# A two-layer block on one core: the down products of the shared gated block as fp32r parts with 512 tokens moving, placed three exponentials behind their rounding

## The chip, the core and the metric

The kernel runs on one core of one Trainium2 chip. The metric is the device time of one execution in microseconds (us), as the median of several runs. A core has five engines that run their own instruction streams in order and meet at semaphores: TensorE (PE, matrix products into PSUM), VectorE (DVE), ScalarE (ACT), GpSimd (POOL) and SyncE (SP, which issues most DMAs).

## What is computed

Two layers over 1024 tokens (batch 2, 512 tokens each) of width 256. The part that matters here is the first layer:

```
xn = layernorm(x)
s  = attention(xn)              # 16 heads of 16, 4 key-value heads, softmax over 512 keys
gate_up = xn @ w_gate_up.T      # 256 -> 2 x 1024
h  = silu(gate) * up            # 1024 wide
f  = h @ w_down.T               # 1024 -> 256, "down"
```

The result f is gated (its tanh is taken and the product scaled by it) and multiplied by the attention output; the sum with x goes to the second layer: a linear attention branch and a mixture of eight experts. All data are float32.

## The kernel before

The time is spent in three parts. A start (to about 45 us) loads, normalizes and projects. A long middle part (to about 221 us) does the attention of the first layer and, mixed into it, the shared gated block. The rest (112 us) is the second layer with the expert tiles.

**The middle part.** Attention runs over 8 units (2 batches x 4 key-value heads) of 4 steps with 4 products each, 128 in all. The plan calls each of these a `prob`: one PE product (L1749) whose 128x512 result ACT turns into exponentials (L1019). They are numbered 1 to 128 here, and "exponential 23" means the `prob` of that number and what stands behind it up to the next. Two PSUM banks serve them in turn, so the product of number q waits for the exponential of number q-2. The four products of a step with the values (`values`, L1759) stand behind the second exponential of the next step. Beside them run the `score` products (L1727) of the next unit, whose row maxima DVE takes (L1292), with two banks as well, and transposes of the second batch's query and key parts (`stack_T`, L1661, copied by ACT at L1027, in exponentials 20 to 42).

**The fill.** The shared block is cut into small items that stand between those of attention. For each batch and each of 8 slices of 128 hidden features: `gate` and `up`, two items each (L1816). An item is three products in fp32r, a rounded form of float32: the operands are split into a high part (rounded by ACT) and a low part (the difference, taken by POOL or DVE), and high x high, high x low and low x high are summed, each with 128 weights columns standing and 512 tokens moving. Then ACT takes the tanh (L1054), DVE makes `gated` (L1337) and `hidden` (L1348), which leaves hT, the hidden values with features in the partitions. After the 8 slices come the `down` items: 4 token tiles per batch x 8 slices, 64 in all, each one plain float32 product (L1829) with 128 tokens of hT standing and the 256 columns of the weight wdn moving. The trace shows such a float32 product as two matrix instructions. At the end of a token tile ACT takes tanh (L1063, 128x256) and DVE the product into gx (L1356, 128x256).

**What sets the order.** `attention_plan` writes one list that PE, ACT and DVE all walk. In it `put` places an item of attention and, ahead of it, items of the fill, as long as the fill is behind a pace (cost units spent, evenly over the 128 exponentials) or while a rough clock of the three engines says that the attention item would wait. POOL has its own code: it clears buffers, prepares the second batch's parts, takes the low parts of xnT (L803) and issues the scatter of rows (L836). SP walks loads and stores.

The lines around the change:

```
for j in range(TB):
    fill += [("down", b * TB + j, i) for i in range(NI)]
...
while fill and (spent < pace - SLACK or spent < pace + AHEAD and clock.start(item) > clock.now["pe"] + 0.1
...
if n >= 2 and hh == 0:
    act.wait_ge(s["values_done"], n - 1)
nc.scalar.activation(probs[:, n % 2, hh, :], ps[:, 2 + hh % 2, :], ACT.Exp,
```

## Time and profile before

| | us |
|---|---|
| median of 3 runs (336.23 to 338.54) | 336.7 |
| the profiled execution's own time | 335.74 |
| its span, first to last instruction | 333.5 |
| PE busy in the span | 317.5 (95%) |
| DVE busy | 223.9 (67%) |
| ACT busy | 161.4 (48%) |
| POOL busy | 66.9 (20%) |

Time outside the span is 2.2 us. In the views, an instruction's duration includes its way through the engine, so two that follow each other closely overlap; what a queue costs is read from the distance between starts, or from a row in which several are merged. The chain of waits gives PE's pieces by that distance. "x8" behind a group counts instructions.

### The profile page before, as it was taken

How to read it: one execution, taken by the hardware profiler on the slowest of the kernel's cores; microseconds unless marked ns; L12 is line 12 of the kernel's file. 1: busy time of each engine (PE TensorE's matmuls, PEld its weight loads, DVE VectorE, ACT ScalarE, POOL GpSimd, SP SyncE). 2: the span in 40 equal slices, each digit the busy share in tenths (PEclk: the TensorE clock that was granted, in tenths of full speed). 3: DMA queues.
4: the chain of work that ended last, by engine and by line, in shares of the span. 5: the costliest groups of instructions: out<-in, count | busy, mean ns of one | idle time of the engine just before them, and what ended most of it. 6: DMA issues, size and time to landing. Idle time of an engine off the chain costs nothing.

```text
span 333.5 us, 4912 instructions
## 1 busy us (share of the span) xinstructions
PE 317.5 (95%) x1646; PEld 189.5 (57%) x1646; DVE 223.9 (67%) x489; ACT 161.4 (48%) x299; POOL 66.9 (20%) x90
## 2 busy tenths in 40 slices
PE   8889999999999999999999999999999999999990
PEld 8655564455555545465455456546654677665650
DVE  3978968695566667868976772129899666454972
ACT  1794457566768455544384455532406622233230
POOL 5009633700030000000000002200321441116132
PEclk9999999999999999999999999999999999999997
DMA  7910073091280650400000005106944896034721
GB/s 221 422 41 0 0 151 108 4 221 37 65 192 3 130 129 9 118 2 2 0 3 1 0 2 206 48 2 249 375 166 115 317 428 264 16 129 145 249 92 36
DMA packets 19867, 39.19 MB, mean 118 GB/s; under 512 B 1698, under 2 KB 15235, under 8 KB 18688
## 3 DMA queue, kind: packets, MB, share of 16 engines
q1 hardware_dynamic: 18448, 35.69, 33.6%
q0 software_dynamic: 1392, 3.15, 2.7%
q8 instruction: 15, 0.25, 0.3%
q14 instruction: 12, 0.10, 0.1%
HBM read 34.02 MB, written 15.22 MB: 148 GB/s over the span
## 4 chain that ended last, share of the span: by engine, by line
PE 83%; DVE 11%; issue 2%; DMA 1%; ACT 1%; POOL 0%; SPq 0%; DVEq 0%; POOLq 0%
PE ps L1816 10%; PE ps L1759 9%; PE ps L1727 9%; PE ps L1829 8%; PE ps L1749 8%; PE ps L1871 6%; PE ps L1887 6%; PE ps L1899 6%; PE ps L1628 4%; PE ps L1564 3%; DVE nmax L1292 3%; PE ps L1661 3%; PE ps L1936 2%; PE ps L1607 2%; PE ps L1861 1%
## 5 line engine op out<-in xcount | busy, mean ns | idle before, releaser
L1292 DVE TENSOR_REDUCE nmax<-ps 128x1 f32<-128x512 f32 x128 | 85.2, 687 | 36.4 <-PE ps L1727 35.3
L1019 ACT ACTIVATE shared<-ps 128x512 f32<-128x512 f32 x128 | 73.8, 594 | 43.1 <-PE ps L1749 42.1
L1727 PE MATMUL ps<-experts 96*128 96x512 bf16 x128 | 47.8, 384 | 2.4 <-DVE experts L1299 1.1
L1749 PE MATMUL ps<-experts 99*128 99x512 bf16 x128 | 48.3, 383 | 0.0
L1829 PE MATMUL ps<-shared,experts 128*128 128x256 f32 x128 | 37.7, 386 | 0.2 <-DVE gated L1337 0.2
L1759 PE MATMUL ps<-shared,experts 128*32 128x512 f32 x256 | 34.1, 605 | 0.3 <-ACT shared L1019 0.3
L1727 PEld LDWEIGHTS ps<-experts 96*128 96x128 bf16 x128 | 12.4, 98 | 37.4 <-DVE nmax L1292 20.3
L1829 PEld LDWEIGHTS ps<-shared,experts 128*128 128x128 f32 x128 | 23.2, 191 | 8.7 <-issue 2.5
L1027 ACT ACTIVATE experts<-ps 96x1024 bf16<-96x1024 bf16 x18 | 18.3, 1021 | 9.8 <-PE ps L1661 9.6
L1628 PE MATMUL ps<-late_weights,xnT 128*128 128x512 f32 (+1 forms) x64 | 22.5, 492 | 0.4 <-DVE shared L1199 0.4
L1871 PE MATMUL ps<-experts,shared 128*128 x88 | 21.0, 382 | 0.8 <-ACT shared L1094 0.8
L1887 PE MATMUL ps<-experts,xsT 128*128 x44 | 20.9, 598 | 0.6 <-ACT xnT L1082 0.6
L836 POOL DMA_INDIRECT slot_rows<-xn,smi x8 | 9.2, 1151 | 57.9 <-DVE smi L1269 56.1
L1899 PE MATMUL ps<-experts,xsT 128*128 x44 | 20.8, 594 | 0.0
L1749 PEld LDWEIGHTS ps<-experts 99*128 99x128 bf16 x128 | 12.4, 98 | 11.5 <-issue 4.9
L1816 PE MATMUL ps<-xnT,late_weights 128*128 128x512 f32 x48 | 18.8, 392 | 0.0
L1871 PEld LDWEIGHTS ps<-experts,shared 128*128 128x128 f32 x88 | 15.9, 190 | 2.8 <-issue 1.0
L1054 ACT ACTIVATE tanh_g<-ps 128x512 f32<-128x512 f32 x16 | 9.5, 596 | 15.7 <-PE ps L1816 15.4
L1088 ACT ACTIVATE xsT<-ps 128x256 f32<-128x256 f32 x12 | 4.6, 384 | 24.1 <-PE ps L1853 24.1
L827 POOL TENSOR_TENSOR router_c<-router,small 128x16 f32<-128x16 f32 x1 | 0.2, 222 | 79.5 <-ACT small L1046 79.5
L1628 PEld LDWEIGHTS ps<-late_weights,xnT 128*128 128x128 f32 x64 | 11.5, 190 | 7.5 <-issue 6.1
L1100 ACT ACTIVATE late_weights<-late_weights 128x256 f32<-128x256 f32 x11 | 4.6, 415 | 21.1 <-DVE late_weights L1489 21.1
(236 smaller groups left out, 541.1 us busy)
## 6 DMA issues: line engine op xcount, KB each, us to landing
experts<-in_experts SPq DMA_DIRECT2D x8, 1536.0 KB, 12.0
slot_rows<-in_empty SPq DMA_DIRECT2D x4, 2080.0 KB, 11.5
shared<-in_wgu SPq DMA_DIRECT2D x2, 1024.0 KB, 9.1
shared<-in_wdn SPq DMA_DIRECT2D x1, 1024.0 KB, 11.4
expert_results<-in_empty SPq DMA_DIRECT2D x1, 1024.0 KB, 6.9
token_rows<-x SPq DMA_DIRECT2D x1, 1024.0 KB, 15.4
token_rows<-gx SPq DMA_DIRECT2D x1, 1024.0 KB, 4.5
shared<-expert_results SPq DMA_DIRECT2D x4, 256.0 KB, 5.6
```

Of the source, the lines that this page charges most:

```text
L1019: nc.scalar.activation(probs[:, n % 2, hh, :], ps[:, 2 + hh % 2, :], ACT.Exp, scale=float(HD) ** -0.5).then_inc(s["exp_done"], 1)
L1027: nc.scalar.activation(dst, src.rearrange("p (h s) -> p h s", h=2), ACT.Copy).then_inc(s["misc_free" if is_late(it) else "stack_copied"], 1)
L1292: nc.vector.tensor_reduce(nmax[:, 4 * t + hh:4 * t + hh + 1], ps[:, m % 2, :], AX, ALU.max, negate=True).then_inc(s["max_done"], 1)
L1628: last = nc.tensor.matmul(bank[:, a, 0:hi - lo], xnT[:, k, P * j:P * j + P], win[:, k, lo:hi], start=k == 0, stop=k == KD - 1)
L1727: nc.tensor.matmul(ps[:, m % 2, :], qs[0:KS, b, GR * g + hh, P * t:P * t + P], ks[0:KS, b, g, :], start=True, stop=True).then_inc(s["score ...
L1749: nc.tensor.matmul(ps[:, 2 + hh % 2, :], ks[0:KM, b, g, P * t:P * t + P], qs[0:KM, b, GR * g + hh, :], start=True, stop=True).then_inc(s[" ...
L1759: last = nc.tensor.matmul(ps[VW * hh:VW * hh + VW, 4, :], vaug[:, TB * b + t, g, :], probs[:, n % 2, hh, :], start=t == 0, stop=t == TB - 1)
L1816: ins = nc.tensor.matmul(ps[:, bk, :], w_parts[w_], x_parts[x_], start=k == 0 and n_ == 0, stop=k == KD - 1 and n_ == 2)
L1829: ins = nc.tensor.matmul(ps[:, bk, 0:D], hT[:, i, P * (j % TB):P * (j % TB) + P], wdn[:, i, :], start=i == 0, stop=i == NI - 1)
L1871: last = nc.tensor.matmul(ps[:, 6, 0:D], hmT[:, i % 2, P * k:P * k + P], Wm[:, bass.ds(base[i] + 2 * KD * EI + D * k, D)], start=k == 0, s ...
L1887: last = nc.tensor.matmul(ps[:, i % 2, :], xsT[:, i % 2, P * k:P * k + P], Wm[:, bass.ds(base[i] + EI * k, EI)], start=k == 0, stop=k == K ...
L1899: last = nc.tensor.matmul(ps[:, 2 + i % 2, :], xsT[:, i % 2, P * k:P * k + P], Wm[:, bass.ds(base[i] + EI * (KD + k), EI)], start=k == 0, ...
```

## The change

- Each `down` item becomes three fp32r products, with 128 columns of a weight part standing and the 512 tokens of a batch moving, as in `gate` and `up`. There are 2 column halves x 8 slices x 2 batches = 32 items. The result has features in the partitions.
- The weight wdn is split: ACT rounds it in two pieces (`round_down`, 128x1024 each), POOL takes the low parts. Each slice of hT is split (`h_parts`, 16 in all): ACT rounds 128x512, POOL takes the low part. Four high parts can be held at a time (PARTS), so from the fifth on the rounding waits for the items of four slices before.
- At a half's end ACT takes tanh of 128x512 and DVE the product, into `gated`. Then `back` items turn the result round: 4 transposes each, 16 in all, and ACT copies 128x512 into gx.
- In the plan, one `h_parts` is placed behind an exponential. A `down` item is let in only 3 exponentials behind the `h_parts` of its values (LAG), and `back` 3 behind the last `down`; while the first item of the fill isn't let in, none is. The pace is that of 120 exponentials instead of 128.
- POOL now walks the list too: its low parts of xnT, the router's centring and the first scatter stand at their places in it.
- Smaller edits: the 0.5 for PE's warm-up products is written by POOL instead of DVE; the bias addition at L1472 is followed by a wait for its own end instead of a wait at a later reader; two semaphores for stored tables are merged.

```diff
-        for j in range(TB):
-            fill += [("down", b * TB + j, i) for i in range(NI)]
-    cost = {"gate": 3, "up": 3, "down": 2}
+        fill += [("down", 2 * b + c, i) for i in range(NI) for c in range(2)]
+        fill += [("back", 2 * b + c, 0) for c in range(2)]
+    cost = {"gate": 3, "up": 3, "down": 3, "back": 3}
...
+    def ready(f):
+        if f[0] == "down":
+            return probs[0] - placed.get(NI * (f[1] // 2) + f[2], probs[0]) >= LAG
+        return f[0] != "back" or probs[0] - placed["down"] >= LAG
...
-        while fill and (spent < pace - SLACK or spent < pace + AHEAD and clock.start(item) > clock.now["pe"] + 0.1
+        while fill and ready(fill[0]) and (spent < pace - SLACK or spent < pace + AHEAD and clock.start(item) > clock.now["pe"] + 0.1
...
+        if coming and item[0] == "prob" and (item[1] % TB, item[2]) not in ((2, 1), (2, 2), (2, 3), (3, 0)):
+            part()
...
-            pace = start + (total - start) * (GR * n + hh + 1) / (GR * STEPS)
+            pace = start + (total - start) * (GR * n + hh + 1) / (GR * STEPS - 8)
...
+            def lower_h(c):
+                pool.wait_ge(s["h_high_ready"], c + 1)
+                b, i = divmod(c, NI)
+                nc.gpsimd.tensor_tensor(h_low(i), hT[:, i, :], h_high(b, i).bitcast(F32), ALU.subtract).then_inc(s["h_low_ready"], 1)
...
+                elif kind == "h_parts":
+                    b, i = divmod(it[1], NI)
+                    if i < PARTS:
+                        act.wait_ge(s["up_ready"], NI * (b + 1))
+                    else:
+                        act.wait_ge(s["down_ready"], 2 * (NI * b + i - PARTS + 1))
+                    bk, n = bank_use[("up", it[1])]
+                    act.wait_ge(free_sem[bk], n + 1)
+                    nc.scalar.activation(h_high(b, i), hT[:, i, :], ACT.Copy).then_inc(s["h_high_ready"], 1)
...
-                    nc.scalar.activation(gated[:, j % 2, 0:D], ps[:, 6 + j % 2, 0:D], ACT.Tanh, scale=0.25).then_inc(s["down_tanh"], 1)
+                    nc.scalar.activation(gated[:, c, :], ps[:, 6 + c, :], ACT.Tanh, scale=0.25).then_inc(s["down_tanh"], 1)
...
-                    ins = nc.tensor.matmul(ps[:, bk, 0:D], hT[:, i, P * (j % TB):P * (j % TB) + P], wdn[:, i, :],
-                                           start=i == 0, stop=i == NI - 1)
+                    if c == 0:
+                        pe.wait_ge(s["h_low_ready"], NI * b + i + 1)
+                    w_parts = [w[:, P * c:P * c + P] for w in (down_high(i), down_low(i))]
+                    h_parts = [h_high(b, i), h_low(i)]
+                    for n_, (w_, h_) in enumerate(((0, 0), (0, 1), (1, 0))):
+                        ins = nc.tensor.matmul(ps[:, bk, :], w_parts[w_], h_parts[h_], start=i == 0 and n_ == 0, stop=i == NI - 1 and n_ == 2)
...
+                    for a in range(2):
+                        for c in range(2):
+                            at_ = P * (2 * half + a)
+                            last = nc.tensor.transpose(ps[:, bk, P * (2 * a + c):P * (2 * a + c) + P], gated[:, c, at_:at_ + P], ident)
+                    last.then_inc(s["back_T"], 1)
...
-            nc.vector.tensor_tensor(qkv1[0][:, 1:TB, :], qkv1[0][:, 1:TB, :],
-                                    bin_b.rearrange("p (o n) -> p o n", o=1).to_broadcast([P, TB - 1, 3 * D]), ALU.add).then_inc(s["bias_added"], 1)
+            chain(nc.vector.tensor_tensor(qkv1[0][:, 1:TB, :], qkv1[0][:, 1:TB, :],
+                                          bin_b.rearrange("p (o n) -> p o n", o=1).to_broadcast([P, TB - 1, 3 * D]), ALU.add))
```

Three places show what moved. First PE around exponentials 23 to 27, before: L1749 is a `prob`, L1727 a `score`, L1661 a `stack_T`, L1829 a `down`, L1759 the `values`.

```order
L1749 MATMUL ps<-experts 128x512
L1727 MATMUL ps<-experts 128x512
L1749 MATMUL ps<-experts 128x512
L1727 MATMUL ps<-experts 128x512
L1829 MATMUL ps<-shared,experts 128x256
L1661 MATMUL ps<-identb,experts 96x128 x8
L1749 MATMUL ps<-experts 128x512
L1727 MATMUL ps<-experts 128x512
L1829 MATMUL ps<-shared,experts 128x256
L1749 MATMUL ps<-experts 128x512
L1759 MATMUL ps<-shared,experts 32x512 x4
```

The same place of the changed program, where L1846, L1824, L1758, L1929 and L1856 stand for these:

```order
L1846 MATMUL ps<-experts 128x512
L1824 MATMUL ps<-experts 128x512
L1846 MATMUL ps<-experts 128x512
L1824 MATMUL ps<-experts 128x512
L1758 MATMUL ps<-identb,experts 96x128 x8
L1846 MATMUL ps<-experts 128x512
L1824 MATMUL ps<-experts 128x512
L1846 MATMUL ps<-experts 128x512
L1929 MATMUL ps<-xn,gx 128x512
L1929 MATMUL ps<-experts,gx 128x512
L1929 MATMUL ps<-xn,shared 128x512
```

The first `down` moved from exponential 24 to 26, and exponentials 23 to 25 have no item of the fill.

Second, ACT at the same exponentials, before: L1019 is an exponential, L1027 the copy of a `stack_T`.

```order
L1027 ACTIVATE experts<-ps 96x1024
L1019 ACTIVATE shared<-ps 128x512 x2
L1027 ACTIVATE experts<-ps 96x1024
L1019 ACTIVATE shared<-ps 128x512 x2
L1027 ACTIVATE experts<-ps 96x1024
```

And changed, with L1123 the exponential, L1131 the copy, L1095 the rounding of a slice of hT:

```order
L1131 ACTIVATE experts<-ps 96x1024
L1123 ACTIVATE shared<-ps 128x512
L1095 ACTIVATE xn<-experts 128x512
L1123 ACTIVATE shared<-ps 128x512
L1095 ACTIVATE xn<-experts 128x512
L1131 ACTIVATE experts<-ps 96x1024
L1123 ACTIVATE shared<-ps 128x512
L1095 ACTIVATE xnT<-experts 128x512
L1123 ACTIVATE shared<-ps 128x512
L1131 ACTIVATE experts<-ps 96x1024
```

Three roundings now stand between the exponentials 23 to 26.

Third, PE at the end of the attention, exponentials 124 to 128, before (L1628 is the first product of the second layer):

```order
L1749 MATMUL ps<-experts 128x512
L1829 MATMUL ps<-shared,experts 128x256
L1749 MATMUL ps<-experts 128x512
L1829 MATMUL ps<-shared,experts 128x256
L1749 MATMUL ps<-experts 128x512
L1759 MATMUL ps<-shared,experts 32x512 x4
L1829 MATMUL ps<-shared,experts 128x256
L1749 MATMUL ps<-experts 128x512
L1829 MATMUL ps<-shared,experts 128x256
L1749 MATMUL ps<-experts 128x512
L1829 MATMUL ps<-shared,experts 128x256
L1759 MATMUL ps<-shared,experts 32x512 x4
```

And changed (L1704 is half of the attention's output product, L1725 stands for L1628):

```order
L1704 MATMUL ps<-wl,experts 128x256 x4
L1846 MATMUL ps<-experts 128x512 x2
L1856 MATMUL ps<-shared,experts 32x512 x4
L1846 MATMUL ps<-experts 128x512 x4
L1856 MATMUL ps<-shared,experts 32x512 x4
L1846 MATMUL ps<-experts 128x512 x2
L1856 MATMUL ps<-shared,experts 32x512 x4
L1725 MATMUL ps<-late_weights,xnT 128x512
```

Exponentials 121 to 128 had one `down` each and now have none.

## Rows read from the trace of the kernel before

**Rows 1.** The page: busy time of the engines, share of the span, instructions
```profile
PE 317.5 (95%) x1646; PEld 189.5 (57%) x1646; DVE 223.9 (67%) x489; ACT 161.4 (48%) x299; POOL 66.9 (20%) x90
```
**Rows 2.** The page: the chain that ended last, by engine
```profile
PE 83%; DVE 11%; issue 2%; DMA 1%; ACT 1%; POOL 0%; SPq 0%; DVEq 0%; POOLq 0%
```
**Rows 3.** Windows: stretch, its length, busy PE PEld DVE ACT POOL, PEclk, DMA
```profile
72.70:79.00 6.30, 6.25 (x48) 3.66 (x45) 5.04 (x10) 3.81 (x7) 0.00 (x0) 1.00 0.55 156
79.00:84.40 5.40, 5.40 (x44) 3.19 (x42) 2.90 (x8) 4.58 (x8) 0.00 (x0) 1.00 0.01 3
84.40:90.30 5.90, 5.90 (x39) 3.38 (x38) 2.45 (x5) 4.47 (x8) 0.00 (x0) 1.00 0.08 24
...
176.90:183.10 6.20, 6.04 (x32) 2.96 (x31) 3.82 (x6) 3.77 (x9) 0.22 (x1) 1.00 0.01 2
183.10:186.90 3.80, 3.67 (x20) 1.25 (x19) 2.83 (x6) 2.28 (x4) 0.00 (x0) 1.00 0.00 0
212.13:221.14 9.01, 8.76 (x49) 4.03 (x48) 0.84 (x2) 5.33 (x10) 0.00 (x0) 1.00 0.01 2
...
10.00:20.00 10.00, 8.15 (x35) 5.25 (x36) 8.09 (x28) 8.31 (x15) 0.00 (x0) 1.00 0.77 315
320.00:333.50 13.50, 5.00 (x24) 3.63 (x22) 5.19 (x11) 2.08 (x5) 5.08 (x5) 0.82 0.12 44
```
**Rows 4.** The chain of waits in order of time: start, us, what
```profile
88.24 0.45 PE ps L1661 x8
...
131.17 0.22 PE ps L1727
...
131.82 2.07 PE ps L1816 x9
...
200.66 2.16 PE ps L1829 x10
...
213.17 0.99 PE ps L1759 x8
...
214.79 0.22 PE ps L1749
...
220.10 0.04 issue
...
235.99 0.87 PE ps L1669 x8
...
241.16 2.46 DVE experts L1472
```
**Rows 5.** Groups of instructions by line and form
```profile
L1063 ACT ACTIVATE gated<-ps 128x256 f32<-128x256 f32 x8 | 3.0, 380 | 3.3 <-PE ps L1829 3.2
L954 ACT ACTIVATE late_weights<-shared 128x1024 fp32r<-128x1024 f32 x3 | 3.1, 1058 | 0.0
L958 ACT ACTIVATE experts<-xnT 128x512 fp32r<-128x512 f32 x2 | 1.2, 621 | 0.0
L803 POOL TENSOR_TENSOR xnT<-xnT,experts 128x512 fp32r<-128x512 f32 x2 | 2.5, 1275 | 28.7 <-ACT experts L958 28.7
L796 POOL TENSOR_TENSOR shared<-shared,xn 128x1024 fp32r<-128x1024 f32 x1 | 2.3, 2342 | 0.0
```
**Rows 6.** The timeline: start, us, what, number merged
```profile
87.65 0.38 PE L1749 MATMUL ps<-experts 99*128 99x512 bf16 x1
88.06 0.60 ACT L1019 ACTIVATE shared<-ps 128x512 f32<-128x512 f32 x1 [1.23 <-PE ps L1749]
205.07 1.08 ACT L1019 ACTIVATE shared<-ps 128x512 f32<-128x512 f32 x2 [0.91 <-PE ps L1749]
84.14 1.01 ACT L1027 ACTIVATE experts<-ps 96x1024 bf16<-96x1024 bf16 x1
85.05 0.59 ACT L1019 ACTIVATE shared<-ps 128x512 f32<-128x512 f32 x1
```
**Rows 7.** One tile's instructions, nres: duration ns min/median/max
```profile
L1327 DVE TENSOR_TENSOR nres<-nmax,mparts x8: 174/175/178, 39.1 to 196.8; 128x16 f32<-128x16 f32 x8
```

170 lines of the change are left out of this document (118 added, 52 removed).

## The prediction

> **What bounds the kernel now.** I read the page first. PE is busy for 317.5 of 333.5 us, DVE for 223.9, ACT for 161.4, POOL for 66.9 [rows 1]. The chain that ended last is PE for 83% and DVE for 11% [rows 2]. So PE's own work is nearly the time, and the question for every edit is how much PE work it takes away and how much new waiting it gives PE.
>
> Busy time alone doesn't tell waiting, since PE's instructions overlap. I therefore priced each item of the list by the chain's distances: a `prob` 0.22, a `score` 0.22, a `stack_T` 0.45, a step's `values` 0.99 [rows 4]. With ten matrix instructions of L1829 in 2.16 us, a `down` (two of them) is 0.43. With nine of L1816 in 2.07, a fp32r item of three is 0.69. Summed over the items that the plan puts there, exponentials 25 to 28 hold 5.2 us of PE work and took 5.40, 29 to 32 hold 5.7 and took 5.90, 21 to 24 hold 5.9 and took 6.30 [rows 3]. PE is full there; 0.2 us in four exponentials is lost, whatever stands in them. Only where the fill is thin is it more: 93 to 100 hold 9.0 and took 6.20 + 3.80 = 10.0 [rows 3].
>
> ACT is the engine to watch. In the same stretches it is busy 3.81 of 6.30, 4.58 of 5.40 and 4.47 of 5.90 us [rows 3], and the change gives it work exactly there.
>
> **The change, part by part.**
>
> *PE work.* Removed: 64 x 0.432 = 27.6 us. Added: 32 items x 0.69 = 22.1, and 16 float32 transposes at 0.109 (eight of L1669 in 0.87 [rows 4]) = 1.7. Sum: **-3.8 us**. The form of the new products (128 columns standing, 512 moving, fp32r) is that of L1816, so this price has its row; I give it 0.5 either way.
>
> *ACT.* A full queue costs less than durations: two exponentials together take 1.08 [rows 6], so 0.49 each and 0.10 once; a `stack_T` copy 0.91 (84.14 to 85.05 [rows 6]). The roundings are 0.62 each [rows 5], 0.52 in a queue. Added: 16 x 0.52 = 8.3, two of 1.06 for the weights [rows 5], about 1.9, four `back` copies 2.0. The tanhs stay even: 8 of 0.38 before [rows 5], 4 of 0.60 now. Together +12 us, which costs nothing by itself and everything where PE waits for the exponential behind it.
>
> *Where ACT is late: exponentials 23 to 26.* Before, a `down` stood in 24 and 25; now nothing does, and three roundings and two copies stand between the exponentials. ACT needs 4 x 0.49 + 3 x 0.52 + 2 x 0.91 = 5.3 us from the copy behind 22 to the rounding in 25; PE's items from 22 to 25 hold 4.4. I walked it, with an exponential starting 0.41 behind its product (87.65 to 88.06) and taking 0.60 [rows 6], and 0.04 for a signal [rows 4]. Zero is the product of 23. The copy of the last `stack_T` holds ACT to 1.1, exponential 23 ends at 1.6, the first rounding at 2.1, 24 at 2.6. PE, free at 1.3, waits for 23 until 1.65, and with product 26 for 24 from 2.1 to 2.65. POOL's part takes 1.28 [rows 5], so the first low part is there at 3.5, and the first `down`, due at 2.9, waits 0.6. That is 1.5 us. Further on, `max_rows` in 29 waits some 0.2 for a copy that the exponentials have pushed back; from 30 to 33 ACT's 5.4 and PE's 5.5 are level and the walk shows no more waits. Sum 1.7. A part of it replaces the 0.2 to 0.4 that four exponentials lose already, so I take **+1.4**. Bounds: 0, if every rounding fell into a gap of ACT, and 16 x 0.52 = 8.3, if PE waited for each (rival A).
>
> *The second half, 93 to 100.* Again there is no fill from 95 to 97. The walk gives waits of 0.2, 0.25 and 0.4 for exponentials and for DVE's maxima and 0.2 for the first low part, 1.05 in all, plus the usual 0.4: 1.45 against 1.0 lost before. **+0.4**.
>
> *Between last `down` and `back`, 46 to 49.* The fill is shut for three exponentials, `back` waits for tanh and DVE's product, and its two copies on ACT stand before exponential 50, for which product 52 waits. **+0.3**, between 0 and 1.
>
> *The tail, 121 to 128.* Eight `down`s left, 3.46 us of work. Before, this stretch to the last `values` took 9.01 [rows 3]. Without a fill it is bound by two banks and ACT: product, 0.41, 0.60 and 0.04 to the next product in that bank make 1.05. From the third product of a step at t: the fourth at t+0.22, the next step's first at 1.05, its second at 1.55 (ACT's queue), `values` 1.77 to 2.76, so 2.76 per step where PE's items are 1.88. From product 121: third at 1.43, 127 at 4.2, 128 at 4.4, its exponential ends at 5.7, `values` at 6.7. 9.0 - 6.7 = 2.3 gained of 3.46 removed here, so **+1.2** is given back. Bounds 0.8 and 1.7.
>
> *113 to 120.* Two `back` stand where PE waited before; +0.1.
>
> *Small edits.* The wait behind L1472 gives up its overlap with the next instruction of DVE, which is on the chain [rows 4]: +0.1. The 0.5 written by POOL and the merged signals stand before and behind longer waits: 0. POOL gets 16 x 1.28 + 2 x 2.34 = 25 us [rows 5] in a part of the program in which it is nearly idle (0.00 us busy in five of the six stretches from 72.7 to 221.1 [rows 3]); what waits for it is PE's `down`, counted above.
>
> Sum: -3.8 + 1.4 + 0.4 + 0.3 + 1.2 + 0.1 + 0.1 = **-0.3 us**. On the profiled execution 335.74 - 0.3 = 335.4; that execution is 1.0 below the median of its runs, 336.7, and so I forecast **336.4**.
>
> A rule that speaks against the change: the DVE instruction of `max_parts` that reads two SBUF operands took 174 to 178 ns in all eight cases [rows 7], with hardly any work of POOL in this part of the program. The Trainium skill, page "SBUF — State Buffer", section "SBUF: two separate sides", says that such a DVE instruction and a GpSimd instruction that reads SBUF exclude each other for a whole instruction. By that rule each `max_parts` that met a subtraction would wait up to its 1.28 us, and with two such meetings the sum would be up to +2.3 instead of -0.3; by the walk POOL has no part in hand where they stand. No row here tests the rule.
>
> **The rivals.**
>
> *A, slower: PE waits for ACT at nearly every rounding.* The mechanism is one queue in which each rounding stands ahead of an exponential, and the rounding itself waits for hT or for a `down` of PE. For it: 4.58 of 5.40 us busy already [rows 3]. Against it: from 30 to 38 the loads are level, not over. Full price 8.3 in place of 1.8 in my two stretches: 336.4 + 6.5 = 342.9. It decides the sign from about half of the roundings (8 x 0.52 = 4.2, 338.8), and is over 1% slower from eleven.
>
> *B, faster: nothing is given back but the tail.* ACT's gaps take the roundings, as they take the copies now. Then -3.8 + 1.2 = -2.6, 334.1; with the tail's loss gone too, 332.9.
>
> *C, POOL is the late one.* Its 1.28 per part and a 2.34 in between [rows 5] hold the `down`s, and while one is shut out all fill is. PE uses a part in 1.38 us of its own products, so POOL keeps up; if it falls behind by one part in each half, 2 x 1.28 = 2.6 more, 339.0.
>
> *D, the clock falls in the tail.* Granted was 1.00, that is 2.4 GHz, with PE busy 8.15 of 10 us and in the stretch of 183.10, and 0.82 only at the end, after PE had stopped [rows 3]. PE's tail will be busy some 70 to 80%. If it fell to 1.2 GHz, 4.8 us of work would double and swallow 2 us of waiting: +2.8, 339.2. The Trainium skill, page "TensorE: Matmul & The Clock Gate", section "A second HAM failure mode: psum-queue depth-cycling", has a kernel whose small gaps between groups made the clock go to and fro; no stretch of this trace does so.
>
> **How the numbers follow.** The forecast 0.64, A 0.12, B 0.15, C 0.05, D 0.04. The forecast's own range is 334.8 to 338.0 (its terms' bounds, and the 0.3% between runs). To leave out no more than 2 in 10 of all cases, the range goes to 333.6 and 339.2. One per cent, about what can be told from no change here, is 3.4 us: faster than 333.3 needs B with the tail's loss mostly gone too, 0.11; slower than 340.1 needs the upper half of A, or C or D with more, 0.10; the rest is 0.79.
>
> **What would show it.** In the changed profile: PE's busy time down by about 3 to 4 us and the new products at 0.23 each; L1095 at 0.62 x 16; waits of `prob` for the exponentials near the first and the second block of roundings; the stretch from product 121 to the end of the last `values` at 6.7 us with waits of PE for ACT of about 2; the time from there to the end as before, 112 us. The prediction is wrong if exponentials 23 to 37 take more than 21 us or less than 19 (the walk says 19.8, for 18.0 of items), if the tail isn't 6.7, or if DVE or POOL ends the waits there instead of ACT.

## The result, and the profile after

The changed kernel takes 338.98 us, the median of 13 runs (337.96 to 339.86). The kernel before, run beside it, takes 336.67, the median of 13 (336.23 to 338.54). The ratio is 1.0059, with a 95% interval of 1.0042 to 1.0077: slower by half a per cent. Forecast was 336.4, no change. The time lies inside the range that was given, but it moved the other way than the forecast of -0.3. Three single runs of the experiments below stand far outside the rest (343.2 us of e6, 408.5 of e14, 1416.4 of e7), and the ratios leave them out. The profiled execution of the changed kernel took 339.86 us, 1.9 of it outside the span; it is the slowest of its 13.

The page of the changed kernel, for [rows 1, 2], with the slices of PE and of the granted clock:

```profile
PE 317.2 (94%) x1630; PEld 184.7 (55%) x1630; DVE 223.3 (66%) x484; ACT 171.8 (51%) x317; POOL 92.1 (27%) x109
PE   8989999998999999999999999889999999999990
PEclk9999999999999999999997999999999999999997
PE 85%; DVE 7%; ACT 3%; issue 2%; POOL 1%; DMA 0%; SPq 0%; POOLq 0%; DVEq 0%; ACTq 0%
```

PE's busy time hardly fell, though its work did, and one slice in the middle has a 7 in the row of the clock, which wasn't forecast. ACT and POOL have joined the chain.

Windows of the changed kernel, for [rows 3]: exponentials 21 to 24, 25 to 28, 29 to 32, 93 to 96, 97 to 100, and the tail. Columns as there.

```profile
73.65:79.68 6.03, 5.79 (x44) 3.26 (x44) 4.37 (x8) 3.60 (x7) 0.92 (x1) 1.00 0.49 139
79.68:86.75 7.07, 6.11 (x43) 3.13 (x42) 2.69 (x7) 5.68 (x10) 3.78 (x3) 1.00 0.01 2
86.75:92.89 6.14, 6.04 (x40) 3.10 (x38) 3.03 (x6) 5.89 (x10) 3.92 (x3) 1.00 0.01 2
178.75:184.62 5.87, 5.75 (x25) 1.90 (x23) 2.32 (x4) 2.97 (x8) 0.22 (x1) 0.71 0.01 2
184.62:191.56 6.94, 6.45 (x30) 2.96 (x30) 4.12 (x7) 4.52 (x10) 5.77 (x5) 1.00 0.00 0
217.08:224.05 6.97, 5.44 (x34) 1.01 (x32) 0.00 (x0) 4.33 (x8) 0.00 (x0) 1.00 0.00 1
```

Read the first three against [rows 3]: 6.03, 7.07 and 6.14 us where before took 6.30, 5.40 and 5.90. In the second, ACT is busy for 5.68 of 7.07. The fourth has a granted clock of 0.71.

Groups of the changed kernel, for [rows 5] (L1095 rounds a slice of hT, L899 is its low part, L893 that of the weights):

```profile
L1095 ACT ACTIVATE xnT<-experts 128x512 fp32r<-128x512 f32 x8 | 5.0, 630 | 0.0
L899 POOL TENSOR_TENSOR experts<-experts,xnT 128x512 fp32r<-128x512 f32 x8 | 10.2, 1282 | 11.8 <-ACT xnT L1095 11.8
L893 POOL TENSOR_TENSOR shared<-shared,gx 128x1024 fp32r<-128x1024 f32 x1 | 2.4, 2378 | 5.5 <-ACT gx L1085 5.5
```

The durations taken from the nearest rows hold: 0.63 for 0.62, 1.28 for 1.28, 2.38 for 2.34.

**A ledger.** Every exponential's product can be found in both traces. So I took the distance between the starts of every fourth one, subtracted the PE work of the items that the list puts there, priced as in the prediction, and subtracted the same for the kernel before. What is left is waiting that the change added (or, below zero, took away), in us; time that PE spends at a lower clock is in it. In all profiles but that of the second experiment exponentials 1 to 16 agree with before to 0.02, so a hundredth means something here. "Forecast" is the prediction's working. The columns e1 to e14 are experiments that follow. The profiles of the changed kernel and of e8 have a fall of the clock in 93 to 100, those of e1, e6 and e14 have none.

```
exponentials  forecast  changed  e1     e6     e8     e14
17-20          0        +0.57   +0.58  +0.59  +0.57  -0.02
21-24          0        +0.20   +0.20  +0.20  +0.19  +0.46
25-32         +1.4      +1.65   +0.26  +1.65  +0.34  +0.34
33-44          0        +0.04   +1.25  +0.05  +0.04  +0.04
45-48         +0.3      +0.52   +0.51  +0.51  +0.51  +0.51
49-92          0        -0.91   -0.88  -0.70  -0.89  -0.69
93-100        +0.4      +2.27   +1.72  +0.66  +1.82  +0.35
101-116        0        +0.10   +0.10  +0.10  +0.10  +0.10
117-120       +0.1      +0.53   +0.53  +0.53  +0.53  +0.53
121-end       +1.2      +1.42   +1.41  +1.41  +1.42  +1.42
waiting       +3.4      +6.39   +5.68  +5.00  +4.63  +3.04
PE work       -3.8      -3.8    -3.8   -3.8   -3.8   -3.8
```

The forecast's waits of 23 to 26 stand in the row of 25 to 32. The column "changed" is the change itself: +6.4 of waiting against -3.8 of work is +2.6 at the last `values`. The experiments take it apart. Behind the last `values` the profiled run of before has 104.8 us to its last product, the changed one 106.0, e10 and e4, which are before with small edits, 105.5 and 105.6. So 0.7 to 0.8 of the 1.2 there is the luck of one profiled run of before, which was 1.0 below its median. With the new list, e5 and e12 have 105.6 as well: behind the last `values` the change costs nothing that these profiles can tell.

### The profile page after: what moved, and what is told of

Read it like the earlier page. It is cut to its first block, busy times and chain, and to the rows that moved or that the text cites. A ratio compares the mean times of both kernels' runs of the same rounds, so it can differ in the third digit from the quotient of the medians.

```text
span 338.0 us, 4929 instructions
## 1 busy us (share of the span) xinstructions
PE 317.2 (94%) x1630; PEld 184.7 (55%) x1630; DVE 223.3 (66%) x484; ACT 171.8 (51%) x317; POOL 92.1 (27%) x109
## 4 chain that ended last, share of the span: by engine, by line
PE 85%; DVE 7%; ACT 3%; issue 2%; POOL 1%; DMA 0%; SPq 0%; POOLq 0%; DVEq 0%; ACTq 0%
PE ps L1913 11%; PE ps L1856 9%; PE ps L1824 8%; PE ps L1846 8%; PE ps L1929 7%; PE ps L1980 6%; PE ps L1996 6%; PE ps L2008 6%; PE ps L1725 3%; PE ps L1661 3%; PE ps L1668 3%; PE ps L1758 2%; PE ps L2045 2%; PE ps L1704 2%; DVE nmax L1392 2%
## 5 line engine op out<-in xcount | busy, mean ns | idle before, releaser
L1123 ACT ACTIVATE shared<-ps 128x512 f32<-128x512 f32 x128 | 73.8, 594 | 45.9 <-PE ps L1846 44.3
L1824 PE MATMUL ps<-experts 96*128 96x512 bf16 x128 | 48.1, 386 | 2.3 <-DVE nmax L1392 1.2
L1846 PE MATMUL ps<-experts 99*128 99x512 bf16 x128 | 48.4, 386 | 1.7 <-ACT shared L1123 0.9
L1856 PE MATMUL ps<-shared,experts 128*32 128x512 f32 x256 | 34.9, 618 | 1.0 <-ACT shared L1123 1.0
L1824 PEld LDWEIGHTS ps<-experts 96*128 96x128 bf16 x128 | 12.4, 98 | 36.0 <-DVE nmax L1392 17.8
L1846 PEld LDWEIGHTS ps<-experts 99*128 99x128 bf16 x128 | 12.3, 99 | 26.0 <-ACT shared L1123 11.8
L1131 ACT ACTIVATE experts<-ps 96x1024 bf16<-96x1024 bf16 x18 | 18.2, 1019 | 9.3 <-PE ps L1758 9.2
L1725 PE MATMUL ps<-late_weights,xnT 128*128 128x512 f32 (+1 forms) x64 | 22.5, 492 | 0.5 <-DVE shared L1300 0.5
L1725 PEld LDWEIGHTS ps<-late_weights,xnT 128*128 128x128 f32 x64 | 11.5, 190 | 7.7 <-issue 6.1
L1461 DVE COPY xs<-ps 128x512 f32<-128x512 f32 x8 | 5.5, 683 | 14.5 <-PE ps L1856 14.5
L1639 DVE TENSOR_TENSOR wl<-gated,ps 128x512 f32<-128x512 f32 x11 | 7.6, 688 | 9.3 <-PE ps L2008 9.3
```

The source lines that it names most:

```text
L1131: nc.scalar.activation(dst, src.rearrange("p (h s) -> p h s", h=2), ACT.Copy).then_inc(s["misc_free" if is_late(it) else "stack_copied"], 1)
L1725: last = nc.tensor.matmul(bank[:, a, 0:hi - lo], xnT[:, k, P * j:P * j + P], win[:, k, lo:hi], start=k == 0, stop=k == KD - 1)
L1824: nc.tensor.matmul(ps[:, m % 2, :], qs[0:KS, b, GR * g + hh, P * t:P * t + P], ks[0:KS, b, g, :], start=True, stop=True).then_inc(s["score ...
L1846: nc.tensor.matmul(ps[:, 2 + hh % 2, :], ks[0:KM, b, g, P * t:P * t + P], qs[0:KM, b, GR * g + hh, :], start=True, stop=True).then_inc(s[" ...
L1856: last = nc.tensor.matmul(ps[VW * hh:VW * hh + VW, 4, :], vaug[:, TB * b + t, g, :], probs[:, n % 2, hh, :], start=t == 0, stop=t == TB - 1)
```

## The experiments

In all experiments except e4 and e10 the base is the changed kernel. Each is compared with the kernel before on the same chip.

**e1_round_on_dve.** All 18 roundings go from ACT's program to DVE's, at the same places of the list.

```diff
-                    nc.scalar.activation(h_high(b, i), hT[:, i, :], ACT.Copy).then_inc(s["h_high_ready"], 1)
+                    nc.vector.tensor_copy(h_high(b, i), hT[:, i, :]).then_inc(s["h_high_ready"], 1)
```

> The changed kernel with all its roundings (16 slices of hT, 2 pieces of the down weights) moved from ACT to DVE, at the same places of the list. Theory Q (PE waits because roundings stand ahead of exponentials in ACT's queue): the 0.6 us more waiting around exponentials 17 to 20 and most of the 1.6 us around 25 to 32 go, and the time falls by 1.5 to 2.5 us, to about 337. Rival P (PE waits for POOL's low parts or for the shut fill, whoever rounds): the first down comes no earlier and the time stays within 0.5 us of 339. If DVE's score maxima are delayed instead, it is slower than 339.

Measured: 339.44 us, ratio 1.0072 (1.0050 to 1.0095). No gain. But the ledger shows two things in one: 25 to 32 lost only 0.26 instead of 1.65, and 33 to 44 lost 1.25 where the changed kernel lost 0.04. In 93 to 100 it lost 1.72 with the clock at 1.00 throughout, where the changed kernel without a fall loses 0.66 (e6). The timeline of e1 tells why (L1428 is the rounding, now DVE's; L899 POOL's low part; the last two rows are 4 us later):

```profile
91.17 1.28 POOL L899 TENSOR_TENSOR experts<-experts,xn 128x512 fp32r<-128x512 f32 x1 [0.36 <-DVE xn L1428]
91.62 1.12 DVE L1428 CAST xn<-experts 128x512 fp32r<-128x512 f32 x1
92.82 1.27 POOL L899 TENSOR_TENSOR experts<-experts,xn 128x512 fp32r<-128x512 f32 x1 [0.36 <-DVE xn L1428]
93.26 1.11 DVE L1428 CAST xnT<-experts 128x512 fp32r<-128x512 f32 x1
...
97.29 0.42 DVE L1428 CAST xnT<-experts 128x512 fp32r<-128x512 f32 x1
97.79 1.28 POOL L899 TENSOR_TENSOR experts<-experts,xnT 128x512 fp32r<-128x512 f32 x1 [2.05 <-DVE xnT L1428]
```

The rounding takes 0.42 us alone and 1.11 where a subtraction of POOL is in hand; it ends 0.28 us behind the end of the subtraction, as all ten roundings of e1 do that meet one. The row maxima queue behind it, and PE's weight loads wait for them (waits of e1, 91 to 96 us: total, times, longest):

```profile
PEld ps L1823 <- DVE nmax L1377: 2.3, 2, 1.5
```

So e1 freed PE from ACT and tied it to DVE. The time that theory Q named, about 337, was missed; the theory isn't refuted by it, since the experiment changed two things.

**e2_pace_128.** The fill is spread over 128 exponentials again.

```diff
-            pace = start + (total - start) * (GR * n + hh + 1) / (GR * STEPS - 8)
+            pace = start + (total - start) * (GR * n + hh + 1) / (GR * STEPS)
```

> The changed kernel with the pace over 128 exponentials instead of 120, so that part of the fill reaches into the last 8 exponentials; the first half's downs start only at exponential 33, behind most of the transposes of the second batch. Theory Q: the roundings of the first half meet fewer transpose copies on ACT and the tail's empty places are used, 1 to 2 us faster than 339. Rival S (what counts is the number of exponentials in which the fill is shut, not where): the shut fill only moves, within 0.5 us of 339.

Measured: 338.98 us, ratio 1.0055 (1.0033 to 1.0077), the changed kernel's own time. Priced by its own list, since the items stand elsewhere, 25 to 28 lost 0.6 instead of 1.4 and the last eight exponentials 1.2 instead of 1.4, but 29 to 32 lost 2.4 instead of 0.3, and the gain of 49 to 92 is gone (+0.4 instead of -0.9). All waits together are 6.2 against 6.4. The `prob` at 88.8 us, the first of 33 to 36, waits for the transfer of the row maxima, as none in the changed kernel for so long (waits of e2):

```profile
PE ps L1846 <- DMA experts<-experts: 1.4, 1, 1.4
```

The pace chooses where the time is lost; it hardly changes how much.

**e3_lag_1.** A `down` may follow its rounding by one exponential.

```diff
-LAG = 3
+LAG = 1
```

> The changed kernel with down and back let in 1 exponential behind instead of 3. Theory Q: PE, in order, then waits for the low part at the first down of each half with nothing ahead of it; the wait of about 0.6 us at the first down of each half grows to 1.5 to 2 us, but the two shut stretches are shorter; 339 to 340. Rival S (the shut fill is the cost): 337.5 or less.

Measured: 342.69 us, ratio 1.0163 (1.0111 to 1.0216). The first `down` comes before POOL's low part is there (waits of e3, 73 to 100 us: total, times, longest):

```profile
PE ps L1929 <- POOL experts L899: 1.8, 1, 1.8
```

By its own list exponentials 21 to 24 lose 2.2 us instead of 0.2 and 93 to 96 lose 3.6 instead of 1.4 (both with the fall of the clock that is told below); all waits together are 8.8 against 6.4. The shut fill of the change is the smaller evil.

**e4_small_edits.** The kernel before with the change's three small edits. Their cores:

```diff
-            nc.vector.memset(tanh_g[:, 0, 0:P], 0.5).then_inc(s["halves_ready"], 1)
+            nc.gpsimd.memset(tanh_g[:, 0, 0:P], 0.5).then_inc(s["halves_ready"], 1)
...
-                dve.wait_ge(s["bias_added"], 1)
...
-            pool.wait_ge(s["x_stored"], 16)
-            pool.wait_ge(s["g_stored"], 16)
+            pool.wait_ge(s["g_stored"], 32)
```

> The kernel before with only three small edits of the change: the 0.5 written by POOL, the wait for the end of the bias addition, the merged semaphores of the stored tables. I expect 0.1 us (the bias wait), so 336.7 to 336.9. Rival: the 0.3 us by which the changed kernel already lags at the first exponential, and the 1 us that it lost among the expert tiles, come from these edits; then 337 to 338.

Measured: 337.59 us, ratio 1.0008 (0.9973 to 1.0042). Its exponentials stand within 0.05 of before's. The small edits cost nothing that can be measured. Its ten runs form two groups, five at 336.3 to 336.8 and five at 338.4 to 340.0, with mean granted clocks of 0.991 to 0.996 and 0.984 to 0.991. Before's runs do the same. Something costs some 2 us in one run and not in another, and it isn't the small edits.

**Where the clock falls.** Windows of the changed kernel behind its `logits`, which stand from 176.3 to 178.5 us (16 products of 8 columns, and 4 more):

```profile
178.00:180.00 2.00, 2.00 (x18) 1.11 (x21) 0.86 (x3) 1.34 (x5) 0.22 (x1) 0.99 0.00 0
180.00:182.00 2.00, 2.00 (x10) 0.33 (x5) 0.01 (x1) 0.91 (x2) 0.00 (x0) 0.50 0.01 2
182.00:184.00 2.00, 2.00 (x7) 1.00 (x6) 1.04 (x2) 0.19 (x1) 0.00 (x0) 0.65 0.01 4
```

0.50 is 1.2 GHz. The `values` there (from 179.86 us) took 1.88 us instead of 1.06. The profiled run of before has 1.00 at its same place.

**e5_round_on_pool, e6_dense_logits, e7_weights_on_pool.** e5 lets POOL make all roundings; e7 only those of the weights (in both at exponentials 19 and 20); e6 only puts unread products into the `logits`.

In e6:

```diff
                                              start=k == 0 and t == 0, stop=False)
+                            if b == 0:
+                                nc.tensor.matmul(bank[:, 256:512], qs[0:KS, 0, 0, 0:P], ks[0:KS, 0, 0, 0:256], start=False, stop=False)
```

In POOL's program, in e5 and e7 (the same lines go from ACT's), with `due(4, 3, ("round_down", 1))` for `due(6, 3, ...)`:

```diff
                 if kind == "round_down":
+                    nc.gpsimd.tensor_copy(down_high1 if it[1] else down_high0, wdn[:, i0:i0 + NI // 2, :].rearrange("p i n -> p (i n)")
+                                          ).then_inc(s["w_high_ready"], 1)
                     lower_down(it[1])
```

And in e5 alone:

```diff
                 elif kind == "h_parts":
+                    nc.gpsimd.tensor_copy(h_high(b, i), hT[:, i, :]).then_inc(s["h_high_ready"], 1)
                     lower_h(it[1])
```

> All 18 roundings (L1085, L1095) leave ACT; POOL makes them itself, each in front of its subtraction, and the second half of the weights is rounded at exponential 20 instead of 28. PE's, DVE's and PE-facing order are those of the changed kernel. Theory Q (the roundings in ACT's queue cost what exponentials 17 to 20 lost, +0.57, 21 to 24, +0.20, and 25 to 28, +1.36, against the kernel before): exponentials 17 to 24 take 11.1 us instead of 11.66, and if POOL kept up, 25 to 28 would be back at 5.8; median about 337.0. Theory P (the parts come one after the other, whoever makes them, and a part that POOL rounds and subtracts takes some 2.5 us instead of 1.28): the 0.77 of 17 to 24 is gained, the first down waits about 1.4 us for POOL instead of 0.6 and the second again, so 25 to 32 lose as much as now; median about 338.1. Also, DVE is free of casts here: if the first experiment fell because DVE's casts of 0.42 took 1.1 beside a subtraction of POOL, none of its long waits for DVE's maxima at exponential 33 comes back (5.7 us there, not 6.9).

> Behind each of the eight small products of the logits that use xnT (128x8 moving, about 0.1 us each) stands a bfloat16 product of 256 columns whose result nobody reads; nothing else is changed. It adds some 0.9 us of PE work (8 x 0.11) just ahead of the place where the clock was granted at 0.50 and 0.65 in the profile of the changed kernel (180 to 184 us). Theory K (the clock falls because PE's array had little to do in the 1.9 us of the small products): the fall is gone in the profile and in nearly all runs, whose mean clocks are .991 and higher instead of .988 in 9 of 13; the median is about 338.1 + 0.9 - 0 = 338.9 or lower and the spread between runs shrinks from 1.9 to below 1 us. Rival (the fall comes by chance, or from what stands ahead of the logits or from the waits behind them): still more than half of the runs at .987 to .989, median 338.98 + 0.9 = 339.9.

> Only the two roundings of the down weights (L1085, 1.05 us each) go from ACT to POOL, at exponentials 19 and 20; the sixteen roundings of the hidden rows stay on ACT. Theory Q by parts: exponentials 17 to 20 take 5.06 instead of 5.63 and 21 to 24 lose 0 to 0.2 less, 25 to 28 stay at about 7.0, 29 to 32 (where the second rounding stood) gain 0 to 0.3; last values 0.6 to 1.0 earlier than in the changed kernel, median 338.98 - 0.8 = 338.2. If the loss of 17 to 20 has another cause (a changed place of a gate item), nothing moves: 339.0.

Measured, e6: 337.83 us, ratio 0.9998 (0.9967 to 1.0029). The eleven runs in the ratio are at 337.4 to 338.5 with clocks of 0.991 to 0.996. The eight products cost 0.2 us (exponentials 89 to 92), not 0.9: most of their time passes beside the small products' weight loads. The clock stays up (windows of e6, same stretches):

```profile
180.00:182.00 2.00, 2.00 (x13) 0.74 (x12) 0.73 (x2) 1.24 (x3) 0.00 (x0) 1.00 0.00 0
182.00:184.00 2.00, 1.41 (x8) 0.50 (x6) 1.90 (x4) 1.45 (x3) 0.26 (x1) 1.00 0.02 6
```

By the ledger, 93 to 100 lose 0.66 instead of 2.27, so the fall costs **1.6 us**. e12 below, with bare `logits` and by chance no fall in its profile, loses 0.68 there, which confirms the price and shows that one profile alone can't show the cure: the groups of runs do. What theory K forecast comes true; by what rule the chip lowers the clock there no run tells. On the same chip 12 of 23 runs of before lay at 338.4 to 339.9, at clocks of 0.984 to 0.988: before has falls too.

e5: 338.00 us, ratio 1.0023 (0.9990 to 1.0057). e7: 342.39, ratio 1.0115 (1.0059 to 1.0172). Both lost in 17 to 20, 2.32 and 3.35 us, and only there was e7 worse than the changed kernel by more than 0.5; in e7's profile the clock fell at 74 us as well as behind the `logits`, in e5's not at all. Neither theory expected that. The timeline of e12 (below) shows its mechanism best: DVE's bfloat16 copy (L1404 in e12), which takes 0.42 us, meets POOL. In e5 it takes 0.93 behind a rounding of POOL and 1.37 behind a subtraction.

With the hidden rows on POOL too, e5 lost 0.81 in 25 to 32 (0.05 and 0.76) instead of 1.65, against theory P. My price for POOL's rounding, that of its subtraction, was too high: it takes 0.61, not 1.28. The group, as it stands in e13:

```profile
L925 POOL CAST xnT<-experts 128x512 fp32r<-128x512 f32 x8 | 4.9, 611 | 0.8 <-PE ps L1930 0.8
```

**e8_hidden_on_pool.** So the sixteen roundings of the hidden rows go to POOL and those of the weights stay on ACT: the last `+` of the diff above alone.

> Only the sixteen roundings of the hidden rows (L1095) go from ACT to POOL, each ahead of its subtraction; the two roundings of the weights stay on ACT at exponentials 19 and 28, as in the changed kernel. If what the fifth experiment showed adds up (its late start came from DVE's copies beside POOL's roundings of the weights, its gain from an ACT without the sixteen roundings), then against the kernel before: exponentials 17 to 20 lose 0.57 and 21 to 24 0.2 as in the changed kernel, 25 to 32 lose 0.8 instead of 1.65, 93 to 100 lose 0.36 instead of 0.66 (without the fall of the clock), and the last values start 1.3 us earlier than in the changed kernel without its clock fall, level with before to within 0.3. Median: 336.6 in runs without the fall, 338.2 in runs with it. Rival (ACT's queue isn't what 25 to 32 wait for, POOL's rate is): no gain there, last values as in the changed kernel, 338.

Measured: **335.72 us**, ratio 0.9964 (0.9941 to 0.9988), faster than both kernels. Part of its distance to before is before's falls: without them before's runs on this chip have a median of 336.2, and the eight runs of e8 without a fall 335.5. 25 to 28 lose 0.04 instead of 1.36, 97 to 100 0.38 instead of 0.82, and not one other row of four exponentials moved by more than 0.02. That is theory Q with one thing changed: ACT's queue cost 1.32 us in the first half. It is also the answer to e1: where the part goes matters as much as that it leaves.

**e9_composite, e10_before_dense.** e9 is e8 with the products of e6 and with the first rounding of the weights at exponential 22, as below; e10 is the kernel before with the products of e6.

```diff
-    due(4, 2, ("round_down", 0))
+    due(5, 1, ("round_down", 0))
```

> The eighth experiment, with the first rounding of the weights moved from exponential 19 to 22, where ACT is busy for 3.8 of 6.3 us, and with the eight unread products between those of the logits. Expected: the 0.57 of exponentials 17 to 20 gone, at most 0.2 more lost in 21 to 24 (POOL must have the low half of the weights, 1.05 + 2.38 us, by the first down at about 81 us), no fall of the clock in any run, median 336.2 with a spread below 1 us: a tie with the kernel before in its undisturbed runs (336.4) and faster than its median wherever its clock falls. If the rounding of the weights at exponential 19 is not what 17 to 20 wait for, its 0.57 stays, 336.7; if POOL is then late for the first down, 337.5.

> The kernel before, with the eight unread products between those of the logits and nothing else. If the fall of the clock is a matter of the logits alone, and belongs to both kernels, this one has no run at a mean clock of .984 to .989 (12 of 23 runs of before had one in the last job) and its median is 336.6, 0.2 above the undisturbed runs of before, where the median of before on such a chip is up to 338.4. If the falls of before have another place (the trace of before shows none), its runs stay in two groups as before's do.

Measured, e9: 341.94 us, ratio 1.0146 (1.0114 to 1.0177). The rounding came at 78.7 us, POOL's low half behind it at 82.1, and PE stood (waits of e9, 79 to 90 us):

```profile
PE ps L1930 <- POOL experts L899: 3.1, 1, 3.1
```

The windows of e9 there:

```profile
82.00:84.00 2.00, 0.00 (x0) 0.00 (x0) 0.00 (x0) 0.57 (x2) 1.92 (x4) 0.66 0.00 0
84.00:86.00 2.00, 1.81 (x7) 1.04 (x11) 0.00 (x0) 0.00 (x0) 1.92 (x4) 0.50 0.00 0
```

25 to 28 lost 5.76: in this execution the clock fell at 82.65 us, while PE stood, and came back at 89.47, so that behind the wait PE worked 5.3 us at 1.2 GHz. This is what rival D had feared of waits, in another place and with more of them. 21 to 24 lost 1.1 instead of 0.2. And **17 to 20 lost 0.57 here too, though no rounding stands there**: what I had put down to the rounding in the expectations up to here isn't the rounding's.

e10: 337.15 us, ratio 0.9988 (0.9965 to 1.0012). All twelve runs are at clocks of 0.992 to 0.996 and within 336.2 and 337.5, while 12 of before's 23 beside them are at 337.9 to 339.2. The fall is before's own, and of the `logits`, though no profile of before has caught it. But the median was to be 336.6, and it lies 0.9 above before's runs without a fall (336.2), where the profile has 0.2 for the products; the rest is unexplained.

**e11_composite_2, e12_round_earlier.** e11 is e8 with the products of e6 and the first rounding of the weights one exponential earlier; e12 is the changed kernel with that one step alone.

```diff
-    due(4, 2, ("round_down", 0))
+    due(4, 1, ("round_down", 0))
```

> Roundings of the hidden rows on POOL (as in the eighth experiment), the eight unread products between those of the logits, and the first rounding of the weights one exponential earlier than in the changed kernel, where ACT stands idle for 0.94 us (69.63 to 70.57 us in its trace), instead of three later. Expected against the kernel before, by exponentials: 17 to 20 lose about 0.1 (the rounding takes 1.05, the gap is 0.94) instead of 0.57, 21 to 24 up to 0.2, 93 to 100 as in the eighth experiment without a fall of the clock, and no run at a mean clock of .991 or lower. Median 335.0, spread below 1 us: faster than both kernels by 0.5% or more. If the loss of 17 to 20 isn't ACT's lateness but, say, the transfer of the row maxima, 0.57 stays: 335.5.

> The changed kernel with nothing but the first rounding of the weights one exponential earlier. ACT theory: exponentials 17 to 20 lose about 0.1 instead of 0.57, 21 to 24 0 to 0.2, everything behind as in the changed kernel; last values 0.5 earlier. Median 338.5, in two groups by the clock. If nothing moves, the 0.57 has another cause.

Measured: e11 336.93 us, ratio 0.9985 (0.9960 to 1.0009); e12 339.08, ratio 1.0058 (1.0028 to 1.0089). In both, 17 to 20 lost 1.6 instead of 0.57, where 0.1 was expected: a gap in ACT's program was the wrong thing to look for. e12's timeline:

```profile
70.72 0.42 DVE L1404 COPY experts<-experts 128x1024 bf16<-128x1024 bf16 x1
71.04 2.36 POOL L893 TENSOR_TENSOR shared<-shared,gx 128x1024 fp32r<-128x1024 f32 x1 [4.00 <-ACT gx L1085]
72.25 1.43 DVE L1404 COPY experts<-experts 128x1024 bf16<-128x1024 bf16 x1
```

The earlier rounding brought the subtraction ahead of DVE's copy, which now takes 1.43. PE's first `stack_T` of batch 1 stands until that copy is done: it starts at 73.79, 0.1 behind its end. In the changed kernel the copy had escaped by chance:

```profile
71.87 0.41 DVE L1404 COPY experts<-experts 128x1024 bf16<-128x1024 bf16 x1
72.19 2.38 POOL L893 TENSOR_TENSOR shared<-shared,gx 128x1024 fp32r<-128x1024 f32 x1 [5.54 <-ACT gx L1085]
```

**e13_pool_and_dense, e14_gate_ahead.** e13 is e8 with the products of e6. e14 adds to it that one `gate` item stands ahead of that `stack_T`, as in the kernel before; the list differs in that one row.

```diff
     def put(item, pace):
+        if item == ("stack_T", 1, 0):
+            clock.run(fill[0])
+            emit()
```

> The eighth experiment (hidden rows rounded by POOL, weights by ACT at exponentials 19 and 28 as in the changed kernel) with the eight unread products between those of the logits. Expected, by exponentials, against the kernel before: 17 to 20 lose 0.57, 25 to 32 0.6, 93 to 100 0.37 without a fall of the clock, last values 0.6 earlier than in before, no run at a mean clock of .991 or lower. Median 335.5 with a spread below 1 us.

> As e13, and one gate item (three products, 0.69 us of PE work) stands ahead of the first stack_T of batch 1 in exponential 20, as in the kernel before, instead of behind it; no other row of the list differs from e13. Theory G (the 0.57 that exponentials 17 to 20 lose in every kernel of this study with the new list, also in the ninth, where no rounding stands there, is PE standing in front of stack_T for DVE's copy L1404, with the gate item behind it): the 0.57 is gone, exponentials 17 to 20 take 5.06 to 5.1 and the median is 335.0. Rival (a late row maximum or ACT's rounding holds the copy itself): the loss stays 0.57 or goes to 21 to 24, 335.5.

Measured: e13 335.70 us, ratio 0.9956 (0.9934 to 0.9978); e14 335.66, ratio 0.9946 (0.9923 to 0.9969). Theory G holds for the place: 17 to 20 go from +0.57 to -0.02, and 0.27 of it is lost again in 21 to 24. The 0.3 that is left can't be seen in the medians, and the 335.0 that was expected wasn't reached. PE's timeline at this place in the kernel before (L1816 is the gate item's last product, L1727 a `score`, L1661 the `stack_T`):

```profile
71.83 0.39 PE L1816 MATMUL ps<-xn,shared 128*128 128x512 f32 x1
72.07 0.39 PE L1727 MATMUL ps<-experts 96*128 96x512 bf16 x1
72.29 0.61 PE L1661 MATMUL ps<-identb,experts 128*96 128x128 bf16 x8
```

In the changed kernel (L1824 the `score`, L1758 the `stack_T`):

```profile
71.63 0.38 PE L1824 MATMUL ps<-experts 96*128 96x512 bf16 x1
72.38 0.62 PE L1758 MATMUL ps<-identb,experts 128*96 128x128 bf16 x8 [0.37 <-issue]
```

And in e14 (L1917 the gate item's last product, L1760 the `stack_T`):

```profile
72.48 0.40 PE L1917 MATMUL ps<-xn,shared 128*128 128x512 f32 x1
72.71 0.61 PE L1760 MATMUL ps<-identb,experts 128*96 128x128 bf16 x8
```

In the changed kernel 0.75 us pass between the starts of the `score` and of the transposes, where 0.22 is its price. The trace calls the wait "issue", but DVE's copy ended at 72.28, 0.1 ahead of the transposes, and the item that moved away was the one that had covered it.

## Why the prediction was wrong, step by step

The waits that the prediction priced are there, by the mechanisms it named, each a little larger than its price. What failed is the sum: the sizes of those waits (+1.4 together), exponentials 17 to 24, which it put at nothing (+0.8), a gain that it didn't see (-0.9), and a granted clock that it took from one execution (0.9 of the medians' 2.3).

- **PE work, -3.8: right.** Pairs of the new products start 0.234 us apart in the median, as those of L1816 do (0.235), and the back transposes 0.109.
- **Where ACT is late, +1.4 (walk 1.7): right.** Measured 1.65 in 25 to 32. The walk's details hold too: `prob` waits for exponentials, 1.2 us in all, and the first `down` waits for POOL's first part, forecast 0.6 (waits of the changed kernel, 79.68 to 86.75 us):

```profile
PEld ps L1846 <- ACT shared L1123: 1.2, 2, 0.9
PE ps L1929 <- POOL experts L899: 0.6, 1, 0.6
```

Its chain from the copy of `stack_T` to the first `down` is the one that was walked, exponential, rounding, low part, product:

```profile
78.98 0.58 ACT shared L1123
79.57 0.53 ACT xn L1095
80.09 0.07 issue
80.16 1.28 POOL experts L899
81.44 0.14 issue
81.58 0.94 PE ps L1929 x3
```

  Exponentials 23 to 37 took 20.66 us, inside the 19 to 21 that I had named, though 0.9 above the walk's 19.8. e8 shows that the cause was the right one.
- **The step that failed, for the clock: rival D's place, and with it the sum's silence on the clock.** "Granted was 1.00" was read from one execution. I looked for a fall in the tail, where PE is busy 5.44 of 6.97 us and the clock stays at 1.00. It fell behind the `logits`, which the change doesn't touch, and costs 1.6 us in the profile. In the first measurement four of before's 13 runs lay above 338.0, and nine of the changed kernel's 13 had clocks of 0.987 to 0.989. So one median is that of runs without the fall, the other of runs with it: 338.98 against 338.1, the median of the four others, about 0.9 of the 2.3 us. Whether the change makes the fall likelier stays open: on the chips of the later comparisons the kernel before had it in 5 of 25, 12, 12, 9 and 12 of 23 runs, and versions with the new list and bare `logits` in 4 of 12 (e8) to 7 of 10 (e2), and, by their clocks of 0.984 to 0.990, in all four of e3. Some of before's runs are at 339.8 to 340.0 with clocks of 0.984, like those of e7, whose profile has two falls; where the second of before would be no profile shows.
- **The step that was missing: exponentials 17 to 24, put at nothing, measured +0.77.** I asked of every `down` where it had moved and not of the other fill. The new pace and costs also moved two `gate` items by one or two rows, one of them behind a `stack_T` that waits for DVE. The comparison of the orders had those rows; I read it from exponential 23 on.
- **93 to 100, +0.4:** 0.66 without the fall. **Between last `down` and `back`, +0.3:** 0.52. **The tail, +1.2 (9.0 to 6.7):** 7.0, so +1.4, with PE behind ACT as the walk had it (waits of the changed kernel, 217.08 to 224.05 us):

```profile
PEld ps L1846 <- ACT shared L1123: 3.0, 4, 1.0
PE ps L1856 <- ACT shared L1123: 1.0, 1, 1.0
```

  The prediction had named a tail other than 6.7 as a sign of being wrong, and it is 0.3 off; the mechanism stands, its size was too small.
- **113 to 120, +0.1:** 0.58; I had let the two `back` fill an old wait of PE there, and most of that wait stayed.
- **Not counted, in the change's favour: 49 to 92, -0.9.** Before lost 0.4 to 0.55 in each of 65 to 68, 85 to 88 and 89 to 92; with the items placed otherwise, 0.1 to 0.3.
- **Small edits, +0.1:** nothing measurable (e4).

The terms without the clock sum to +1.0 instead of -0.3: 5.0 of waiting less 0.2 for e6's own products, against 3.8. Every estimated wait was too low, the large ones by a fifth: together 3.4 was put down and 4.8 measured. Of the two that nobody estimated the gain (0.9) is only a little larger than the loss (0.77). So the sign of the forecast is lost without the clock already, by the sizes of the waits. Runs without a fall agree with such a sum where there are many: e6 is 1.3 us above before's on its chip (sum 1.2), e12 2.2 above (2.0), e8 0.7 below (0.6). The changed kernel's own four are 1.7 above before's 336.4, 0.7 more than its 1.0, and that stays open. **Rival A** (ACT late at nearly every rounding) fell: between 33 and 44 nothing was lost. **Rival C** would have needed 1.28 more per half; POOL ended one wait of 0.6. **Rival B** fell with 25 to 32. The measured 339.0 lies only in the outer range, which was widened for rivals; the terms' own bounds end at 338.0, about where the runs without a fall are.

**The rule on DVE and POOL.** By the runs, an instruction of DVE that copies or casts from SBUF to SBUF doesn't run beside a subtraction or a cast of POOL that began before it: 0.42 became 1.11 and 1.43, 2.21 for the one rounding of e1 that met POOL's part of the weights (2.37), and 0.93 behind the cast in e5, each time with its end 0.28 us behind POOL's. The Trainium skill, page "SBUF — State Buffer", section "SBUF: two separate sides", says that whichever of the two starts first keeps the shared port for its whole instruction, and names two kinds of DVE instruction: those with two SBUF inputs (against a GpSimd instruction that reads SBUF), which I weighed, and those in a two-port performance mode, which I passed over. The runs agree with that rule if these copies and casts are of the second kind; no view shows an instruction's mode. The `max_parts` instructions that I weighed never met POOL in the changed kernel, as the walk had it; for [rows 7], the changed kernel:

```profile
L1427 DVE TENSOR_TENSOR nres<-nmax,mparts x8: 174/175/176, 39.4 to 201.9; 128x16 f32<-128x16 f32 x8
```

## What to carry to other kernels

When a planner's costs or pace change, compare the whole order of the engine that bounds the kernel, not the part that was meant to move: a filler item that slips behind a waiting instruction costs its whole cover. Give a new helper operation to the engine that has nothing in the critical queue, and check what it shares with its neighbours: the same sixteen roundings cost 1.3 us more on ACT than on POOL in the first half and 0.3 in the second, and on DVE (with the two of the weights) 1.1 and 1.4. And read the granted clock of all runs before trusting a difference of half a per cent: one fall cost 1.6 us, more than the change without it (1.0 by the ledger), and eight unread products, 0.2 us in the profiles, took it away.

The best version, e14, is at 0.9946 (0.9923 to 0.9969) of the kernel before, about 1.8 us; of that 0.8 is the list (3.8 less 3.0 of waiting), the rest the clock. Against before's runs without a fall on the same chip (median 336.55) it is 0.9 faster. e13 is as fast within what the runs can tell.

## What the runs showed of the hardware that I had not expected

- The granted clock fell to 0.50 while the profile had PE busy in every window around it (2.00 of 2.00), behind 20 products of 8 columns; with eight products of 256 columns between them the times and mean clocks of 12 runs of e10 and of the 11 of e6 show no fall. Busy time in the profile doesn't foretell it, and it comes in some executions of one program and not in others.
- Those eight products took 0.2 us together where half a `score` each, 8 x 0.11, was the price. In the stretch of the bare `logits` the weight loads are busy 2.24 of 2.27 us, which fits small products that wait for theirs and leave room:

```profile
176.33:178.60 2.27, 2.27 (x22) 2.24 (x21) 1.75 (x6) 0.57 (x1) 0.00 (x0) 1.00 0.00 0
```
- POOL casts 128x512 from float32 to fp32r in 0.61 us and 128x1024 in 1.04, as fast as ACT (0.63 and 1.05), while its subtractions take 1.28 and 2.38.
